# Two attention layers on one core: every group of layer 1 in two float32r parts, its sums doubled, seeded by copies and joined by a transfer

## The reference

```python
# layer 0                                        # layer 1
g, theta = Wg x + bg, Wt x + bt                  q, k, v = Wq x + bq, Wk x + bk, Wv x + bv
phi = Wp x + bp              (64 channels)       (128 channels)
y = softmax(theta' phi) g                        y = softmax(q' k / sqrt(128)) v
x = W y + bw + x                                 out = x + y
```

## Time and profile before

| | us |
|---|---|
| median of 3 runs (lowest, highest) | 3255.3 (3254.9, 3256.21) |
| the profiled execution | 3254.69 |
| its span | 3252.9 |
| PE, POOL busy | 3204.8, 3020.9 |
| DVE, ACT busy | 2088.1, 1897.1 |
| a block of layer 0, of layer 1, in a steady stretch | 43.1, 56.9 |

### The profile page before, as it was taken

One profiled execution on the slowest core, in us unless ns is written; L12 is line 12 of the kernel. 1 busy time (PEld: TensorE's weight loads), 2 busy tenths in 40 slices (PEclk: granted clock), 3 DMA queues, 4 the chain that ended last, 5 costly groups with the idle time before them and its releaser, 6 DMA issues. The chain is left out here.

```text
span 3252.9 us, 38831 instructions
## 1 busy us (share of the span) xinstructions
PE 3204.8 (99%) x13636; PEld 2199.8 (68%) x13636; DVE 2088.1 (64%) x3036; ACT 1897.1 (58%) x2473; POOL 3020.9 (93%) x1611
## 2 busy tenths in 40 slices
PE   8999999999999999999999999999999999999997
PEld 5555555557777775555777776555577777777775
DVE  5555555556777765555777776555577777777773
ACT  5555455556666665455666665555566666666665
POOL 6988999998999999999999999999899999999998
PEclk9999999999999999999999999999999999999999
DMA  1000000004665640000565664000066675657566
GB/s 52 26 20 26 23 27 26 27 23 94 136 136 119 143 101 27 26 27 27 107 142 114 141 131 101 22 22 26 27 136 136 125 144 115 128 117 143 117 136 120
DMA packets 91922, 271.45 MB, mean 83 GB/s; under 512 B 10192, under 2 KB 10192, under 8 KB 91728
## 3 DMA queue, kind: packets, MB, share of 16 engines
q0 software_dynamic: 55296, 201.35, 32.2%
q1 hardware_dynamic: 36432, 67.62, 6.8%
HBM read 50.83 MB, written 16.78 MB: 21 GB/s over the span
## 5 line engine op out<-in xcount | busy, mean ns | idle before, releaser
L924 DVE TENSOR_REDUCE piece_max<-rough 128x1 f32<-128x512 f32 x2032 | 1314.7, 683 | 657.1 <-PE rough L510 646.9
L1046 POOL TENSOR_TENSOR p_lo<-probs,p_hi 128x1024 fp32r<-128x1024 f32 x448 | 1191.4, 2712 | 64.4 <-ACT probs L835 54.0
L385 POOL TENSOR_TENSOR sums<-sums,probs 128x1024 f32<-128x1024 f32 x448 | 1067.1, 2382 | 110.4 <-ACT probs L841 70.3
L941 DVE TENSOR_TENSOR probs<-scores,shift_rows 128x1024 f32<-128x1024 f32 x512 | 626.2, 1223 | 470.1 <-PE scores L543 466.9
L841 ACT ACTIVATE probs<-scores 128x1024 f32<-128x1024 f32 x512 | 521.0, 1024 | 654.3 <-PE scores L537 653.5
L834 ACT ACTIVATE p_hi<-probs 128x1024 fp32r<-128x1024 f32 x448 | 474.5, 1059 | 558.6 <-DVE probs L941 558.4
L510 PE MATMUL rough<-keys_a,qry_a 128*128 128x512 f32 x2032 | 714.2, 420 | 11.3 <-POOL keys_a L1046 3.2
L835 ACT ACTIVATE probs<-probs 128x1024 f32<-128x1024 f32 x512 | 535.7, 1046 | 88.8 <-DVE probs L941 88.8
L510 PEld LDWEIGHTS rough<-keys_a,qry_a 128*128 128x128 f32 x2032 | 366.4, 188 | 276.5 <-DVE piece_max L924 151.9
L1089 POOL DMA_DIRECT2D sent_sums<-probs x384 | 442.3, 1152 | 0.2 <-issue 0.2
L539 PE MATMUL scores<-qry_a,keys_a 128*128 128x512 f32 x1024 | 425.7, 416 | 0.0
(11 more groups left out here) (94 smaller groups left out, 3172.6 us busy)
## 6 DMA issues: line engine op xcount, KB each, us to landing
sent_sums<-probs POOLq DMA_DIRECT2D x384, 512.0 KB, 4.9
x_q<-x SPq DMA_DIRECT2D x32, 256.0 KB, 2.7
x_res<-x SPq DMA_DIRECT2D x32, 256.0 KB, 2.9
mid<-mid_new SPq DMA_DIRECT2D x32, 256.0 KB, 2.2
x_kv<-mid SPq DMA_DIRECT2D x32, 256.0 KB, 2.7
x_q<-mid SPq DMA_DIRECT2D x32, 256.0 KB, 2.7
x_res<-mid SPq DMA_DIRECT2D x32, 256.0 KB, 4.5
out<-result SPq DMA_DIRECT2D x32, 256.0 KB, 3.4
```

Of the source, the lines that this page charges most:

```text
L385: eng.tensor_tensor(sums[:], sums[:], probs[:, slot(st, s)], ALU.add).then_inc(s_plus, 1)
L924: nc.vector.reduce_max(piece_max[:, t, c:c + 1], src, AX.X).then_inc(s_reduced, 1)
L941: nc.vector.tensor_tensor(probs[:, slot(st, s)].rearrange("p (h c) -> p h c", c=QB), scores[:, s % 2].rearrange("p (h c) -> p h c", c=QB), ...
L1046: nc.gpsimd.tensor_tensor(dst, w, rd(hi), ALU.subtract).then_inc(done, 1)
```

## The change

**Values.** Groups 2 and 3 are split like the others: `WHOLE` and `v_vals` go, `v_hi` and `v_lo` hold 8 chunks.

**Sums.** `sent_sums` has two copies, by the block's parity. SP copies groups 0 and 1 into it with plain transfers (`copy_probs`), POOL sends groups 2 to 15, and the two halves are joined by one more adding transfer in the next block (`join`, at `JOIN_AT`, group 2 in layer 1 and 3 in layer 0); the fold follows at group 4 (5), the denominators at 6, the reciprocal rows at 9 and the finish at 10, each one group later than before.

**Pieces.** In layer 1 the pieces stand around the scores: of two, one is ahead; of three, two are.

**Queries.** `q_whole` goes. ACT copies to `qry_a` once, in front of its last exp; DVE makes `qry_b` at once, from PSUM, at the block's end. The second piece waits for it.

**Late stage.** The chunks, now 8 and not 7 to split, are spread over groups 6, 9, 12 of block 55 and 0, 2, 5, 8, 11 of block 56. `diag` now shares the place of `rdiag`.

```diff
-FOLD_AT = {None: (None, None), 0: (1, 1), 1: (3, 2)}
-DEN_AT = 5
-RDEN_AT = 8
+JOIN_AT = (3, 2)
+FOLD_AT = ((1, 1), (5, 4))
+DEN_AT = (5, 6)
+RDEN_AT = (8, 9)
...
-MOVES_AT = ({6: 0, 8: 1, 10: 2, 12: 3, 14: 4}, {1: 5, 3: 6, 5: 7})
+MOVES_AT = ({6: 0, 9: 1, 12: 2}, {0: 3, 2: 4, 5: 5, 8: 6, 11: 7})
...
+            def copy_probs(st, s):
+                sp.wait_ge(s_whole, whole_of(st.g, s))
+                if s == COPIED[0]:
+                    sp.wait_ge(s_fold, st.g - (st.prev == 1))
+                settle(sp)
+                sp.dma_start(sent_sums[:, st.parity, s], probs[:, slot(st, s)]).then_inc(s_copied[s], 16)
...
+                    if m == 1:
+                        pe.wait_ge(l_q, st.g + 2)
...
-                if s >= LAG and st.layer == 1 and s - LAG in WHOLE:
-                    if st.opens:
-                        pe.wait_ge(h_v, st.b * BLOCKS + WHOLE_CHUNK + 1)
-                    value_group(st, s - LAG)
-                elif s >= LAG and st.layer == 1:
+                if s >= LAG and st.layer == 1:
                     halved_values(st.b, st.opens, st.g, st.nth, st.parity, s - LAG)
...
-            def take_q_whole(g, layer, src):
+            def take_q_hi(g, layer, parity, src):
                 act.wait_ge(p_q, g + 1)
-                if not (isinstance(g, int) and g == 0):
-                    act.wait_ge(l_q, g)
-                copy(q_whole[:], src, (TH_B, Q_B)[layer])
...
+            def split_q(g, layer, parity, src):
+                dve.wait_ge(h_q, g + 1)
+                nc.vector.scalar_tensor_tensor(out=qry_b[:, parity], in0=src, scalar=(TH_B, Q_B)[layer],
+                                               in1=rd(qry_a[:, parity]), op0=ALU.add,
+                                               op1=ALU.subtract).then_inc(l_q, 1)
...
+            def join(nth, parity):
+                all_sent(pool, nth)
+                settle(pool)
+                nc.gpsimd.dma_start(sent_sums[:, parity, 0], sent_sums[:, parity, 1],
+                                    accum_op=ALU.add).then_inc(s_joined, 16)
```

More of the change, by code:

```diff
@@ L50 @@
 V_LO_AT = 13
-WHOLE_CHUNK = 1
-WHOLE = (2, 3)
-HALVED = tuple(s for s in range(16) if s not in WHOLE)
-SEEDS = 2
-SEED_AT = {2: 0, 3: 2}
-SENT = tuple(range(4, 16))
+COPIED = (0, 1)
 class Stage:
@@ L468, in block_program @@
                     load_q(st.g + 2, *st.next_q)
+                if st.layer == 1:
+                    for s in COPIED:
+                        copy_probs(st, s)
                 if st.prev is not None:
@@ L1018, in block_program @@
                     if s == DIAG_AT and st.nxt is not None:
-                        shift(st.g + 1, 1 - st.parity)
-                    if st.layer == 1 and st.nxt is not None and at[s] == 3:
+                        shift(st.g + 1)
+                    here = at[s] if st.nxt is not None else 0
+                    ahead = here // 2 + here % 2 if st.layer == 1 else here
+                    for _ in range(ahead):
                         reduce_piece(st.pieces + m, pieces[m], two_banks(m))
@@ L1066, in split_held @@
                 pool.wait_ge(h_v, n + 1)
[L1067 removed]
+                lo_part(v_lo[:, c], held(c), v_hi[:, c], l_v)
             def split_probs(st, s):
```

221 lines of the change are left out of this document (92 added, 129 removed).

## The result

The changed kernel takes 3274.27 us (median of 4 runs, 3272.88 to 3274.86), the kernel before 3255.10 in the same session (4 runs, 3254.87 to 3256.21). The ratio is 1.0058, 95% interval 1.0040 to 1.0075: **slower by 19 us**, where the prediction was 3230 us, 25 us faster, with a range of 3220 to 3250. The profiled execution took 3272.88, with a span of 3271.1.

A forecast was written before the change was run, and what follows sets the result against it. PE was taken to set the pace, with POOL close behind in layer 1. Values -25.1, queries +4.5, late stage -3.5, end -1.0 and start -0.6 summed to -25.7, giving 3230 us; range 3220 to 3250.

The forecast's parts named there:

- Values of groups 2 and 3 split: Layer 1 blocks: splitting both float32 groups saves PE 0.81 us a block (0.44 + 0.37), -25.1 us over 31 blocks.
- Pieces around the scores: Layer 1 groups with three pieces: one piece still waits for a reduction; 0, bounds -0.3 and +0.5 us a block.
- Queries: Start of 28 layer 1 blocks: PE waits for `qry_a` and restarts slower, +0.16 us each, +4.5 in all.
- copies: Sums of groups 0 and 1: group 0's copy has 8.7 us to land before the first send; cost 0.
- transfer engines: Layer 1 blocks: added sends and copies fit, share 0.92 at the bound; 0, up to +0.5 us a block.
- POOL's ledger: Layer 1 block: 6.53 us of work added, 8.48 removed, leaving POOL 52.65 us in a block of 56.2.
- Rival A: Layer 1 blocks: pieces, restart and landings cost 0.5 us more in each of 28, 3244 us; chance 0.14.
- Rival B: Layer 1 blocks: POOL and its transfers are the true pace, blocks stay at 56.9 us, 3250 in all; chance 0.10.
- C: Layer 1 denominators: the join lands late, so the fold is late and PE waits; slower, 3272 us; chance 0.08.
- D: Queries in layer 1: DVE's split waits out one of POOL's, 2.35 us; +38 us, 3268; chance 0.04.
- Late stage: Block 56 (from 2787.48): PE's 2.9 us wait for POOL goes, chunks being spread; -3.5 us, bounds -4.1 and +2.
- Ends: Last block, paced by POOL and its transfers, -1.0 us; at the start one ACT copy leaves the path, -0.6.

The follow-up runs named there:

- experiment 3: Changed kernel with the pieces behind the scores and fold, denominators, finish and key projections one group earlier, both as before: 3257.65 us, ratio 1.0008.
- 5: Experiment 3's kernel with the third rough piece of a group at the group's end, behind the values: 3252.48 us, ratio 0.9989.
- 6: Kernel before with only the third rough piece of a group moved to the group's end, behind the values: 3259.28 us, ratio 1.0011.
- experiment 4: Changed kernel with three pieces in group 11 instead of group 10: 3265.7 us in one run.
- 7: 5's kernel; POOL adds the sums ahead of layer 0 blocks, held values move behind the fold, block 63's denominators two groups later: 3245.10 us, ratio 0.9971.
- ninth: 7's kernel with denominators, their rows and the finish one group later in blocks 49 to 62: 3246.95 us, ratio 0.9976.
- eleventh: 7's kernel with denominators, their rows and the finish one group later in blocks 56 to 62 only: 3244.81 us, ratio 0.9966.
- experiment 1: Changed kernel with layer 1's pieces behind the scores again, only the third of three ahead: 3264.82 us, ratio 1.0027.

## Why the prediction was wrong, by its own steps

- **What bounds the kernel** held: PE paces layer 1, with POOL 2 to 3 us behind it, before and after.
- **Values of groups 2 and 3 split, 0.81 us a block**: the rows were read rightly, and the step from them failed. "It lies on the path, as PE has no other wait in these blocks to fall into" was false. The first group gave its gain less a restart of some 0.1 behind the denominators: split, it takes 1.46 us there (experiment 3) and not 1.36. The second's 0.37 stood ahead of a piece that could not start sooner. The prediction read that piece's longer hold (0.34) as the float32 group's doing, and it was the mark of a piece that had waited, by its weight load for 0.57 us. Measured: 0.33 us a block with a piece ahead of group 7 (experiment 3), 0.68 without one (5 against 6). Rows 10 had 151.9 us of such waits in the whole span; in the block of 1021.26 they are three, 1.3 us together. The prediction looked at their longest (0.8) and not at where they stood.
- **Pieces around the scores, taken as 0, bounds -0.3 and +0.5**: the worst step. In a steady block it is +0.4 against the pieces behind (57.10 against 56.71), inside the bounds, 0.16 of it the queries' term. The bounds were made for DVE's reductions alone. That a piece waits for keys too, once per chunk, was not looked at; in blocks 23 and 39 it made 15.1 of the 18.2 us, with the projections' move by one group (9 to 10 and 11 to 12), which the prediction did not price at all. Of the steps moved by a group it followed the fold and the denominators, not the keys.
- **Finish and normalise in group 10** were named inside the bound of +0.5 and measure 0.65 to 0.72 us in each of 12 blocks (experiment 4). In blocks 24 and 40, where the same move puts them beside layer 0's pieces, the changed kernel loses 1.5 us each. In block 24 one piece takes 1.1 of it, an idle time of 0.8 us for a reduction that stands behind the normalise and the finish, and the restart; the prediction had no term for them.
- **Queries, +0.16**, **copies, 0**, **join, 0**, **transfer engines, 0**, **POOL's ledger** (52.65, measured 53.76): as forecast in the steady blocks. "In layer 0 the scores still stand first, so nothing waits" was not true of block 0, where a piece waits 0.4 us for DVE's split of the queries. The copies land after 3.7 us at the median. The Trainium skill ("DMA: Bandwidth & Descriptors", Anatomy of one DMA), whose rule is for transfers issued by GpSimd, gave an estimate of 3.2 for these, which SyncE issues; the measured 3.7 decides, and the sum does not hang on it.
- **Rival A**, small waits that add up, is what group 10 shows (0.65 us a block with key projections). **Rival B** fell: POOL is busy for 53.8 of 57.1 us. **Rivals C and D** did not come true in the changed kernel's steady blocks. C's mechanism, the late fold, is real one group earlier: in experiments 3, 5 and 7 it costs 2 to 5 us in a block at the seams. D is refuted by 64 splits of 0.75 us. The rule of the Trainium skill cited with it ("SBUF — State Buffer", Who interferes with whom) agrees with this trace as far as it goes: these 64 splits have one SBUF operand, and no run has them with two.
- **Late stage, -3.5**: measured 0.0. The 2.2 us of waits for the held values' low parts are gone as meant, but the same splits of POOL, now ahead of the fold, make the sum late, and PE waits for it:

```profile
PE acc_out L583 <- POOL total L350: 2.6, 1, 2.6
```

  Two of these splits, 1.26 us each by the distance of starts, stand ahead of the fold, which begins 20.2 us into the block and not 17.5. POOL's sum of work for block 56 came to 54.6, and it was busy for all 59.5 of it. Its timeline fills most of the rest: 17 splits of probabilities start in the block and not 16, as one was left over from block 55 (2.35 us), and some 3 us are starts that lie further apart than their work, which the overlapping records hide. With the denominators' wait gone (ninth and eleventh kernels) the block still takes 59.4 and 59.7, paced by POOL.
- **Ends, -1.0 and -0.6**: +0.2 and -0.4. In block 63 no pieces stand between the groups, so they take 2.7 us instead of 3.2. The denominators come up sooner, and PE waited 2.4 us for the sum.
- **Block 55, +1.5**: the pieces ahead of the scores reach the next stage's last keys too early there as well, a wait of 1.3 us with ACT as the releaser; with the pieces behind (experiment 1) it takes 55.52.

Added: +15.1 (keys), +3.0 (layer 0 behind layer 1), +1.5 (55), +1.3 (other layer 0 blocks), less 2.7 from everything else, make the +18.2. Without blocks 23 and 39 the change would stand at +3.1, not at the forecast's -25.7: seeing the keys' wait alone would not have saved the prediction. The larger part of the miss is the gain that the steady blocks did not give.

Of the 1.3 us of the other layer 0 blocks 0.3 each in 15, 31 and 47 are no loss: it is the next block's first piece, which now stands ahead of the first scores of layer 1, and so inside the length of the block before. Another 0.4 is block 0's wait for the queries.

**What stays open**: why, in blocks without key projections, the pieces around the scores are better with the denominators at group 6 and worse with them at 5; it was read from waits on reductions, but no run takes DVE's share in it apart. Why block 56 takes 3.0 us more with the pieces behind the scores (experiment 1) is open too. DVE's split of the queries was not tried alone either.

## What to carry to other kernels

When an instruction is moved up or down a queue, list every semaphore that it waits on, the rare ones too (here a key chunk that is new in two blocks of 64), and work out for the block with the least slack when each arrives. A fast replacement for a slow piece of work gains only what the next instruction can use. If the one behind it starts late or holds the engine longer than its kind does, it was waiting, and the slow work hid that. Prices at the seams (first and last block, change of layer) have to be summed apart: the steady blocks gave 8 us in the eleventh experiment, and the unmended seams of the changed kernel cost more than twice that.

## What the runs showed of the hardware

A wait of 6.1 us on PE left it 8.2 us behind: the granted clock was 0.50, the lower level, from 1182.79 to 1189.62, where ten matmuls started 0.43 us apart, and 1.00 from there on, with starts 0.227 apart again. Waits under 0.5 us left the clock at 1.00 and still cost 0.11 us each at the restart, visible as 0.34 instead of 0.227 between two starts. Plain copies of 512 KB inside SBUF land after 3.7 us at the median, the adding ones of the same size after 5.1, in the same blocks with the transfer engines busy for 0.82.
